# Routing drain and wide attention stage of a two-layer decoder: row positions computed right behind their expert choice, one scatter put ahead of a root, and gathered norms applied ahead of copies

## The chip, the cores and the metric

The kernel runs on one core of one Trainium2 chip. The metric is the device time of one execution in microseconds (us); before the change the median of three runs is 362.25 us. The core's engines work side by side, each with its own queue of instructions in program order: TensorE (PE, matmuls; PEld is its weight load), VectorE (DVE), ScalarE (ACT), GpSimd (POOL) and SyncE (SP, here only for DMAs). They meet through semaphores. An instruction whose semaphore is not there holds up all that stands behind it on its engine.

## The reference, cut to what matters

Two decoder layers over x of 16 sequences of 64 tokens, 128 features: self-attention, cross-attention and a feed-forward block in each, with a residual and a LayerNorm behind each of the six. The first feed-forward block routes every token to two of eight experts:

```python
x = _layernorm(x + _L0_attn_ref(x, ...))       # 16 heads of 8, RoPE, causal
x = _layernorm(x + _L0_xattn_ref(x, ctx, ...)) # 16 heads of 8, masked
x = _layernorm(x + _L0_ffn_ref(x, gate_w, wg, wu, wd))
x = _layernorm(x + _L1_attn_ref(x, W_qkv, W_out))   # 16 heads of 64 ("wide")
x = _layernorm(x + _L1_xattn_ref(x, ctx, ...))
x = _layernorm(x + _L1_ffn_ref(x, ...))        # ternary weights, GELU

def _moe_forward(x, gate_w, wg, wu, wd):       # _L0_ffn_ref, E=8, I=512, K=2
    logits = x_flat @ gate_w.T
    top_v, top_i = jax.lax.top_k(logits, K)
    probs = softmax(top_v)
    combine = einsum('tk,tke->et', probs, one_hot(top_i, E))
    for each expert e:
        hidden = silu(x_flat @ wg[e].T) * (x_flat @ wu[e].T)
        out += combine[e][:, None] * (hidden @ wd[e].T)
```

## The kernel before, in words

The 1024 tokens are eight tiles of 128 tokens (NT = 8), two sequences each. Everything is f32. Each attention stage is a software pipeline over its eight tiles. `stream_pe`, `stream_act`, `stream_dve` and `stream_pool` write, for every step j, what each engine does for the tiles j, j-1, ... j-5 at their different points of the stage. `pre` is the stream of the two first attention stages (a0, a1), `post` the stream of the three last (wide, a2, fc). Between them stands the routed feed-forward block `moe`.

**The drain.** When the stream `pre` is out, the last tiles of cross-attention a1 (S[5], S[6], S[7], the tiles 5 to 7) are finished by four hand-written lists, `drain_pe`, `drain_act`, `drain_dve` and `drain_pool`, in which the first steps of `moe` are woven in. Their order is the order on the engines. For a tile i of a1:

- `va_pe` weighs V with the probabilities (L566, 32 matmuls into the bank B_Y). It waits until `y_dve` of the tile before has read that bank.
- `y_dve` on VectorE makes the reciprocals and normalises y (L676 `rs`, L680 `ysb`).
- `y_pe` transposes y (L582), `y_act` copies it to `yT` on ScalarE (L632), `o_pe` projects it (L586).
- `r_dve` adds the residual (L388 `R`) and takes the statistics (L324, L326 `mv`).
- `rsqrt_pool` makes the root on GpSimd (L331 `ve`, L333 `rstd`); `ln_dve` applies the norm (L337 `X`).
- `moe.x_pe` and `moe.x_act` turn the normed tile into `XT` (L1446, L1450).

Routing goes in groups of two tiles, k = 0 to 3. `logits_pe` and `logits_act` (L1365, L1371) make the expert logits. `choose` on VectorE finds the two best experts (L1379 `top` to L1396 `before`). `rank_pe` counts with small matmuls how many tokens chose each expert before this one (L1412, L1414). `place` on VectorE turns that into the row of each token (L1424 `rk`, L1427 `pm`, L1429 `posf`, L1431 `pos`). `scatter` on GpSimd (L1438) sends a tile's tokens to their rows in the DRAM tensor `routed_rows`, one indirect DMA for each of the two choices, 16 in all. `weights_pe` and `weights_copy` (L1348, L1353) transpose the 24 expert weight blocks in between. The last group's counts give the map of the blocks (`map_dve`, L1464 to L1485).

**The routed block.** SP waits for all 16 scatters, then loads blocks of 128 rows to XG (L1508). Up to 23 blocks go through gate, up and down matmuls (L1550, L1558, L1581). GpSimd then gathers the two rows of each token back (`gather`, L1701, into the memory of KB); `combine` on VectorE adds them to the residual and takes statistics (L1711 to L1719), `rsqrt` on GpSimd makes the root (L1724, L1726), and `apply` on VectorE writes the normed tile (L1731).

**The start of the wide stage.** `combine` and `apply` of the tiles 2 to 7 are put into the first steps of the stream `post` by the hook `post_dve`, and the transposes of these tiles by `post_pe` (`turn_pe`, L1741) and `post_act` (L1747). In step j VectorE does the softmax's maximum and subtraction of tile j-2 (`max_dve`, L403, L409), its share of the copies of Q, K (L877, `qkw_copies`, tile j-1) and V (L877, `vw_copies`, tile j-2) out of PSUM, then the hook, then the rest. TensorE's step is: scores (`s_pe`, L827), projections (`qkw_pe`, L801), V (`v_pe`, L813), the transposes of the probabilities (`t_pe`, L429, which wait for `shares_pool`, L906, on GpSimd), and at the end of the step the hook `turn_pe`.

Of the kernel before, what the change touches and what calls it, by code (L numbers as in the profile page):

```python
# [78 lines left out]
def decoder_kernel(nc, A, out):  # L79
    with ExitStack() as ctx:  # L80
# [1167 lines left out]
        def stream_dve(dve, tiles, extra, last):  # L1248
            for j in range(last):
                y = at(tiles, j - 5)  # L1250
                if y:
                    y.stage.y_dve(dve, y)
                t = at(tiles, j - 3)
                hidden = t and isinstance(t.stage, Ternary)
                if hidden:
                    t.stage.sum_dve(dve, t)
                ternary, others = [], []
                for x in turned(tiles, j):
                    (ternary if isinstance(x.stage, Ternary) else others).append(x)
                for x in others:  # L1260
                    x.stage.ln_dve(dve, x)
                if t and not hidden:
                    t.stage.sum_dve(dve, t)
                v = at(tiles, j - 2)
                if v:
                    v.stage.max_dve(dve, v)
                b, q = at(tiles, j), at(tiles, j - 1)
                if q:
                    q.stage.qkw_copies(dve, 1, q)
                w = at(tiles, j - 4)  # L1270
                if w:
                    w.stage.w_copies(dve, 1, w)
                if v:
                    v.stage.vw_copies(dve, 1, v)
                extra(dve, j, False)
                if w:
                    w.stage.ya_dve(dve, w)
                for r in summed(tiles, j):
                    r.stage.r_dve(dve, r)
                for x in ternary:  # L1280
                    x.stage.ln_dve(dve, x)
                if b:
                    b.stage.qk_dve(dve, b)
                extra(dve, j, True)
# [469 lines left out]
        moe = Routed(a1.norm)  # L1754
# [67 lines left out]
        def drain_pe(pe):  # L1822
            moe.logits_pe(pe, 1)
            a1.y_pe(pe, S[5])
            a1.t_pe(pe, S[7])
            a1.o_pe(pe, S[5])
            a1.va_pe(pe, S[6])
            moe.rank_pe(pe, 1)
            a1.y_pe(pe, S[6])
            weights_pe(pe, 0, 1)  # L1830
            a1.va_pe(pe, S[7])
            a1.o_pe(pe, S[6])
            moe.x_pe(pe, 4)
            weights_pe(pe, 1, 2)
            moe.x_pe(pe, 5)
            weights_pe(pe, 2, 3)
            moe.logits_pe(pe, 2)
            weights_pe(pe, 3, 4)
            a1.y_pe(pe, S[7])
            weights_pe(pe, 4, 5)  # L1840
            a1.o_pe(pe, S[7])
            weights_pe(pe, 5, 7)
            moe.rank_pe(pe, 2)
            moe.x_pe(pe, 6)
            weights_pe(pe, 7, 9)
            moe.x_pe(pe, 7)
            weights_pe(pe, 9, 10)
            moe.logits_pe(pe, 3)
            weights_pe(pe, 10, 13)
            moe.rank_pe(pe, 3)  # L1850
            weights_pe(pe, 13, 3 * EXPERTS)

        def drain_act(act):
            moe.logits_act(act, 1)
            a1.y_act(act, S[5])
            a1.pt_act(act, S[7])
            a1.y_act(act, S[6])
            weights_act(act, 0, 1)
            moe.x_act(act, 4)
            weights_act(act, 1, 2)  # L1860
            moe.x_act(act, 5)
            weights_act(act, 2, 3)
            moe.logits_act(act, 2)
            weights_act(act, 3, 4)
            a1.y_act(act, S[7])
            weights_act(act, 4, 7)
            moe.x_act(act, 6)
            weights_act(act, 7, 9)
            moe.x_act(act, 7)
            weights_act(act, 9, 10)  # L1870
            moe.logits_act(act, 3)
            weights_act(act, 10, 3 * EXPERTS)
            act.activation(warm[:, 0:1], half[:, :], ACT.Silu)

        def drain_dve(dve):
            a1.y_dve(dve, S[5])
            moe.choose(dve, 1)
            a1.r_dve(dve, S[5])
            a1.y_dve(dve, S[6])
            a1.ln_dve(dve, S[4])  # L1880
            moe.place(dve, 1)
            a1.ln_dve(dve, S[5])
            a1.r_dve(dve, S[6])
            a1.y_dve(dve, S[7])
# [6 lines left out]
            moe.place(dve, 3)  # L1891

        def drain_pool(pool):
            a1.rsqrt_pool(pool, S[5])
            moe.scatter(pool, 2, 0)
            moe.scatter(pool, 2, 1)
            a1.rsqrt_pool(pool, S[6])
            moe.scatter(pool, 3, 0)
            moe.scatter(pool, 3, 1)
            a1.rsqrt_pool(pool, S[7])  # L1900
            for t in range(4, NT):
                for r in range(2):
                    moe.scatter(pool, t, r)
# [13 lines left out]
                moe.turn_act(act, TURNED[j, late])  # L1917

        def post_dve(dve, j, late):
            if not late and j in (2, 3):  # L1920
                for t in (2 * j - 2, 2 * j - 1):
                    moe.apply(dve, t)
            if late and j in (1, 2, 3):
                for t in (2 * j, 2 * j + 1):
                    moe.combine(dve, t)
# [153 lines left out]
```

## Time and profile before

| | |
|---|---|
| median of 3 runs | 362.25 us (361.87 to 362.48) |
| the profiled execution | 363.17 us |
| its span, first to last instruction | 361.2 us |
| mean granted TensorE clock | 0.971 |
| TensorE busy | 320.9 us, 89% |
| VectorE busy | 231.3 us, 64% |
| GpSimd busy | 202.8 us, 56% |
| ScalarE busy | 182.7 us, 51% |

Times in the trace count from the span's start. The stages follow each other: the two first attention stages to about 97 us, the drain to about 119 us, the routed block to about 194 us, the gathers and the start of the wide stage to about 229 us, and the rest to 361 us. Busy shares are means over all of them; what a change in one stretch is worth has to be read there, from the wait that ended last.

### The profile page before, as it was taken

How to read it: one execution, taken by the hardware profiler on the slowest of the kernel's cores; microseconds unless marked ns; L12 is line 12 of the kernel's file. 1: busy time of each engine (PE TensorE's matmuls, PEld its weight loads, DVE VectorE, ACT ScalarE, POOL GpSimd, SP SyncE). 2: the span in 40 equal slices, each digit the busy share in tenths (PEclk: the TensorE clock that was granted, in tenths of full speed). 3: DMA queues.
4: the chain of work that ended last, by engine and by line, in shares of the span. 5: the costliest groups of instructions: out<-in, count | busy, mean ns of one | idle time of the engine just before them, and what ended most of it. 6: DMA issues, size and time to landing. Idle time of an engine off the chain costs nothing.

```text
span 361.2 us, 10722 instructions
## 1 busy us (share of the span) xinstructions
PE 320.9 (89%) x4182; PEld 262.6 (73%) x4182; DVE 231.3 (64%) x554; ACT 182.7 (51%) x384; POOL 202.8 (56%) x289
## 2 busy tenths in 40 slices
PE   2969999999888399999995688999999799999993
PEld 2647667777677299999994656798888577767673
DVE  2698987788876023583333379855566667877685
ACT  2457666777558633232322243645444466667651
POOL 2856998887777235553313776422122565476785
PEclk9998999999999789999998599999999999999999
DMA  6799999000011201111101110000000000000001
GB/s 187 224 311 242 296 326 321 14 2 3 24 35 48 62 26 51 47 46 45 44 24 33 43 35 25 4 2 2 4 2 4 3 2 3 4 2 2 2 24 36
DMA packets 37052, 23.55 MB, mean 65 GB/s; under 512 B 4228, under 2 KB 34956, under 8 KB 36876
## 3 DMA queue, kind: packets, MB, share of 16 engines
q1 hardware_dynamic: 35692, 20.16, 19.7%
q0 software_dynamic: 1024, 2.10, 2.0%
q8 instruction: 34, 0.56, 0.6%
q10 hardware_dynamic: 288, 0.62, 0.5%
q14 instruction: 14, 0.11, 0.1%
HBM read 15.13 MB, written 7.73 MB: 63 GB/s over the span
## 4 chain that ended last, share of the span: by engine, by line
PE 73%; DVE 12%; issue 4%; DMA 3%; POOL 3%; ACT 2%; SPq 1%; POOLq 0%; ACTq 0%; DVEq 0%
PE banks L801 8%; PE banks L429 8%; PE banks L1550 6%; PE banks L1558 6%; PE banks L1581 6%; PE banks L566 5%; PE banks L539 5%; PE banks L845 4%; PE banks L813 4%; PE banks L511 3%; PE banks L861 2%; PE banks L523 2%; PE banks L827 2%; PE banks L1026 2%; PE banks L582 2%
## 5 line engine op out<-in xcount | busy, mean ns | idle before, releaser
L690 POOL TENSOR_TENSOR KB<-KT,cst 128x512 f32<-128x512 f32 x48 | 49.3, 1048 | 8.2 <-DVE KT L650 5.9
L438 ACT ACTIVATE PT<-banks 128x512 f32<-128x512 f32 x64 | 34.9, 595 | 24.4 <-PE banks L429 23.2
L403 DVE TENSOR_REDUCE mx<-banks 128x16 f32<-128x1024 f32 x32 | 38.6, 1206 | 11.7 <-PE banks L550 10.1
L1573 DVE TENSOR_TENSOR PT<-banks,PR 128x512 f32<-128x512 f32 x23 | 15.9, 690 | 41.8 <-PE banks L1558 37.5
L1538 POOL COPY U<-WALL 128x1024 f32 x21 | 21.9, 1042 | 36.5 <-PE banks L1558 36.3
L877 ACT ACTIVATE U<-banks 128x512 f32<-128x512 f32 x44 | 26.1, 597 | 30.6 <-PE banks L801 15.3
L331 POOL TENSOR_SCALAR ve<-mv 128x1 f32<-128x1 f32 x40 | 9.2, 230 | 49.4 <-DVE mv L326 49.0
L429 PE MATMUL banks<-cst,PR 128*128 128x128 f32 x256 | 35.5, 283 | 0.6 <-POOL PR L906 0.6
L419 ACT ACTIVATE PR<-PR 128x1024 f32<-128x1024 f32 x32 | 33.8, 1058 | 3.5 <-DVE PR L413 3.2
L801 PE MATMUL banks<-XT,WQKV 128*128 128x128 f32 x256 | 33.0, 291 | 0.4 <-ACT XT L1747 0.4
L801 PEld LDWEIGHTS banks<-XT,WQKV 128*128 128x128 f32 x256 | 31.5, 204 | 1.1 <-ACT XT L1747 0.7
L429 PEld LDWEIGHTS banks<-cst,PR 128*128 128x128 f32 x256 | 28.3, 143 | 4.3 <-POOL PR L906 1.5
L539 PE MATMUL banks<-KB,QS 64*64 64x512 f32 x192 | 27.1, 630 | 3.2 <-DVE PR L413 2.2
L413 DVE TENSOR_TENSOR PR<-banks,mx 128x1024 f32<-128x1024 f32 x24 | 29.4, 1224 | 0.8
L566 PE MATMUL banks<-VB,PT 128*64 128x18 f32 x768 | 26.7, 212 | 0.0
L566 PEld LDWEIGHTS banks<-VB,PT 128*64 128x64 f32 x768 | 24.3, 138 | 3.0 <-issue 0.5
L1550 PE MATMUL banks<-XGT,U 128*128 128x128 f32 x184 | 25.3, 282 | 0.0
L1558 PE MATMUL banks<-XGT,U 128*128 128x128 f32 x184 | 25.1, 281 | 0.0
L1701 POOL DMA_INDIRECT KB<-routed_rows,pos x16 | 15.9, 991 | 16.4 <-DMA routed_rows<-YS 12.3
L333 POOL TENSOR_TENSOR rstd<-ve,half 128x1 f32<-128x1 f32 x40 | 23.1, 578 | 3.3
L1581 PE MATMUL banks<-WALL,PT 128*128 x184 | 24.4, 276 | 0.6 <-DVE YS L1589 0.6
L906 POOL TENSOR_TENSOR PR<-PR,rs 128x1024 f32<-128x1024 f32 x8 | 15.2, 1904 | 17.1 <-DVE rs L916 17.0
(190 smaller groups left out, 722.4 us busy)
## 6 DMA issues: line engine op xcount, KB each, us to landing
routed_rows<-zero SPq DMA_DIRECT2D x1, 4544.0 KB, 21.5
WALL<-in_L_ffn_wg_dram SPq DMA_DIRECT2D x8, 256.0 KB, 5.1
WALL<-in_L_ffn_wu_dram SPq DMA_DIRECT2D x8, 256.0 KB, 5.3
WALL<-in_L_ffn_wd_dram SPq DMA_DIRECT2D x8, 256.0 KB, 5.7
U<-in_L_attn_W_qkv_dram SPq DMA_DIRECT2D x1, 1536.0 KB, 22.8
XG<-routed_rows SPq DMA_DIRECT2D x23, 64.0 KB, 1.8
routed_rows<-YS SPq DMA_DIRECT2D x23, 64.0 KB, 1.6
cst<-shape_constants ACTq DMA_DIRECT2D x1, 537.0 KB, 4.4
```

Source lines behind the costliest of these rows:

```text
L403: dve.tensor_reduce(mx[:, n % 2, :], s, AX.X, ALU.max).then_inc(self.max.sem, 1)
L413: dve.tensor_tensor(PR[:, n % 2, :].rearrange("q (h k) -> q h k", k=SEQ), s, bc(mx[:, n % 2, :], 2, SEQ), ALU.subtract).then_inc(self.sub. ...
L419: act.activation(p, p, ACT.Exp, scale=self.scale).then_inc(self.exp.sem, 1)
L429: t = pe.transpose(PS[:, B_PT + m, P * (r % 4):P * (r % 4 + 1)], PR[:, n % 2, P * r:P * (r + 1)], ident)
L438: act.activation(PT[:, n % 2, 4 * m:4 * m + 4, :].rearrange("p r q -> p (r q)"), PS[:, B_PT + m, :], ACT.Copy).then_inc(self.pt.sem, 1)
L539: pe.matmul(PS[q, B_S + g, :], QS[f, n % 3, q], KB[f, n % 2, b].rearrange("p h k -> p (h k)"), start=True, stop=False)
L566: m = pe.matmul(PS[64 * b:64 * b + 64, B_Y, w * r:w * (r + 1)], PT[:, n % 2, r, 64 * b:64 * b + 64], VB[:, n % 3, r, b].rearrange("p a e - ...
L690: pool.tensor_tensor(KB[:, n % 2, b], bc(KT[:, n % 2, b, :], 1, 8), bc(cst[:, C_HEAD:C_HEAD + 8], 2, SEQ), ALU.mult).then_inc(self.kb.sem, 1)
L801: m = pe.matmul(PS[:, bank, P * k:P * (k + 1)], WQKV[:, f // 2, P * u:P * (u + 1)], XT[:, P * i:P * (i + 1)], start=True, stop=True)
L1550: m = pe.matmul(PS[:, j % 2, P * c:P * (c + 1)], WE[:, j % 3, 0, P * c:P * (c + 1)], XGT[:, j % 3, :], start=True, stop=True)
L1558: m = pe.matmul(PS[:, 2 + j % 2, P * c:P * (c + 1)], WE[:, j % 3, 1, P * c:P * (c + 1)], XGT[:, j % 3, :], start=True, stop=True)
L1581: m = pe.matmul(PS[:, 7, 0:P], HT[:, j % 2, c, :], WALL[:, e, 2, P * c:P * (c + 1)], start=(c == 0), stop=(c == CH - 1))
```

## The change

In the drain, `place(dve, 1)`, the four steps that give the rows of tiles 2 and 3, moves from behind `ln_dve` of tile 4 to directly behind `choose(dve, 1)`. On TensorE `va_pe` of tile 7 moves ahead of `y_pe` of tile 6 and the first weight block; `y_pe` of tile 7 moves one weight block forward, and `rank_pe` of group 2 one weight block forward. ScalarE's list follows. On GpSimd the first scatter of tile 2 moves ahead of the root of tile 5. In the wide stage, `apply` of tiles 2 and 3 (step 2) and 4 and 5 (step 3) moves from behind VectorE's copies to ahead of them, directly behind `max_dve`. No operation is added or removed.

```diff
                 if v:
                     v.stage.max_dve(dve, v)
+                if tiles is post and j in (2, 3):
+                    for g in (2 * j - 2, 2 * j - 1):
+                        moe.apply(dve, g)
                 b, q = at(tiles, j), at(tiles, j - 1)
                 if q:
                     q.stage.qkw_copies(dve, 1, q)
...
             moe.rank_pe(pe, 1)
+            a1.va_pe(pe, S[7])
             a1.y_pe(pe, S[6])
             weights_pe(pe, 0, 1)
-            a1.va_pe(pe, S[7])
             a1.o_pe(pe, S[6])
...
             moe.logits_pe(pe, 2)
-            weights_pe(pe, 3, 4)
             a1.y_pe(pe, S[7])
-            weights_pe(pe, 4, 5)
+            weights_pe(pe, 3, 5)
             a1.o_pe(pe, S[7])
-            weights_pe(pe, 5, 7)
+            weights_pe(pe, 5, 6)
             moe.rank_pe(pe, 2)
+            weights_pe(pe, 6, 7)
...
             a1.y_dve(dve, S[5])
             moe.choose(dve, 1)
+            moe.place(dve, 1)
             a1.r_dve(dve, S[5])
             a1.y_dve(dve, S[6])
             a1.ln_dve(dve, S[4])
-            moe.place(dve, 1)
             a1.ln_dve(dve, S[5])
...
         def drain_pool(pool):
+            moe.scatter(pool, 2, 0)
             a1.rsqrt_pool(pool, S[5])
-            moe.scatter(pool, 2, 0)
             moe.scatter(pool, 2, 1)
...
         def post_dve(dve, j, late):
-            if not late and j in (2, 3):
-                for t in (2 * j - 2, 2 * j - 1):
-                    moe.apply(dve, t)
```

Line numbers of the kernel after the change are 3 higher from the first edit on. VectorE's queue in the drain before, from the end of `choose(1)` (L1396) to the norm of tile 5:

```order
L1396 TENSOR_TENSOR before<-before,chosen 128x8 x2
L388 TENSOR_TENSOR R<-banks,XR 128x128
L324 BN_STATS stats<-R 128x6
L326 BN_AGGR mv<-stats 128x2
L676 RECIPROCAL rs<-banks 128x16
L680 TENSOR_TENSOR ysb<-banks,rs 128x128
L337 TENSOR_SCALAR X<-R,mv,rstd 128x128
L1424 TENSOR_TENSOR rk<-banks,cst 128x16
L1427 TENSOR_TENSOR pm<-OH,rk 128x32
L1429 TENSOR_REDUCE posf<-pm 128x4
L1431 CAST pos<-posf 128x4
L337 TENSOR_SCALAR X<-R,mv,rstd 128x128
```

And after the change:

```order
L1399 TENSOR_TENSOR before<-before,chosen 128x8 x2
L1427 TENSOR_TENSOR rk<-banks,cst 128x16
L1430 TENSOR_TENSOR pm<-OH,rk 128x32
L1432 TENSOR_REDUCE posf<-pm 128x4
L1434 CAST pos<-posf 128x4
L388 TENSOR_TENSOR R<-banks,XR 128x128
L324 BN_STATS stats<-R 128x6
L326 BN_AGGR mv<-stats 128x2
L676 RECIPROCAL rs<-banks 128x16
L680 TENSOR_TENSOR ysb<-banks,rs 128x128
L337 TENSOR_SCALAR X<-R,mv,rstd 128x128 x2
```

The four steps of `place` now stand ahead of the residual of tile 5 and the `ysb` of tile 6. TensorE's queue in the same place before, from the end of `rank_pe(1)` to the transpose of tile 5:

```order
L1414 MATMUL banks<-before,onesb 128x8
L582 MATMUL banks<-cst,ysb 128x128
L1348 MATMUL banks<-cst,WALL 128x128 x4
L566 MATMUL banks<-VB,PT 64x18 x16
L586 MATMUL banks<-WT,yT 128x128
L1446 MATMUL banks<-cst,X 128x128
L1348 MATMUL banks<-cst,WALL 128x128 x4
L1446 MATMUL banks<-cst,X 128x128
```

And after the change:

```order
L1417 MATMUL banks<-before,onesb 128x8
L566 MATMUL banks<-VB,PT 64x18 x16
L582 MATMUL banks<-cst,ysb 128x128
L1351 MATMUL banks<-cst,WALL 128x128 x4
L586 MATMUL banks<-WT,yT 128x128
L1449 MATMUL banks<-cst,X 128x128
L1351 MATMUL banks<-cst,WALL 128x128 x4
L1449 MATMUL banks<-cst,X 128x128
```

The `va_pe` matmuls of tile 7 (L566, 16 in the program, 32 passes in the trace) now stand first. VectorE's queue in step 2 of the stream `post` before, where R and X in L1731 are the residual sums and the normed tiles 2 and 3:

```order
L403 TENSOR_REDUCE mx<-banks 128x16
L409 TENSOR_TENSOR PR<-banks,mx 128x2x8x64
L877 COPY U<-banks 128x512 x2
L1731 TENSOR_SCALAR X<-R,mv,rstd 128x128 x2
L1711 SCALAR_TENSOR_TENSOR R<-KB,pk,X 128x128
```

And after the change:

```order
L403 TENSOR_REDUCE mx<-banks 128x16
L409 TENSOR_TENSOR PR<-banks,mx 128x2x8x64
L1734 TENSOR_SCALAR X<-R,mv,rstd 128x128 x2
L877 COPY U<-banks 128x512 x2
L1714 SCALAR_TENSOR_TENSOR R<-KB,pk,X 128x128
```

The two norms change places with the two copies.

## Rows read from the trace of the kernel before

**Rows 1.** The page: the span, and engines' busy time with share and instructions.

```profile
span 361.2 us, 10722 instructions
PE 320.9 (89%) x4182; PEld 262.6 (73%) x4182; DVE 231.3 (64%) x554; ACT 182.7 (51%) x384; POOL 202.8 (56%) x289
```

**Rows 2.** The chain that ended last, drain: start us, us, what.

```profile
99.15 0.30 DVE R L388
...
100.16 0.30 DVE ysb L680
...
101.28 1.04 PE banks L566 x32
102.32 0.42 PE banks L586 x2
...
113.71 0.26 DVE pos L1431
...
118.09 2.21 DMA routed_rows<-X,pos
```

**Rows 3.** The timeline, 98 to 103 us: start, us, engine, line, operation [idle before].

```profile
99.43 0.17 PE L1414 MATMUL banks<-before,onesb 128*128 128x8 bf16 x1
100.51 0.33 PE L582 MATMUL banks<-cst,ysb 128*128 128x128 f32 x1 [0.92 <-DVE ysb L680]
100.74 0.17 DVE L1424 TENSOR_TENSOR rk<-banks,cst 128x16 f32<-128x16 f32 x1
100.88 0.37 ACT L632 ACTIVATE yT<-banks,bvc 128x128 f32<-128x128 f32 x1 [2.01 <-PE banks L582]
101.48 0.34 DVE L337 TENSOR_SCALAR X<-R,mv,rstd 128x128 f32<-128x128 f32 x1
102.83 0.29 DVE L388 TENSOR_TENSOR R<-banks,XR 128x128 f32<-128x128 f32 x1 [1.02 <-PE banks L586]
```

**Rows 4.** The timeline of GpSimd in the drain.

```profile
100.08 0.22 POOL L331 TENSOR_SCALAR ve<-mv 128x1 f32<-128x1 f32 x1 [0.41 <-DVE mv L326]
...
101.86 1.09 POOL L1438 DMA_INDIRECT routed_rows<-X,pos  x1 [0.91 <-DVE pos L1431]
...
107.94 0.28 POOL L331 TENSOR_SCALAR ve<-mv 128x1 f32<-128x1 f32 x1 [0.26 <-DVE mv L326]
...
114.30 0.96 POOL L1438 DMA_INDIRECT routed_rows<-X,pos  x1 [0.30 <-DVE pos L1431]
```

**Rows 5.** Stretches: busy (x count) of PE, PEld, DVE, ACT, POOL, PEclk, DMA, GB/s.

```profile
26.00:28.00 2.00, 2.00 (x17) 1.58 (x14) 1.97 (x4) 0.76 (x3) 2.00 (x3) 0.50 1.13 312
...
126.00:128.00 2.00, 2.00 (x11) 2.00 (x11) 0.00 (x0) 0.60 (x1) 0.00 (x0) 0.50 0.11 33
128.00:130.00 2.00, 2.00 (x19) 2.00 (x18) 0.69 (x1) 0.79 (x2) 1.04 (x1) 0.93 0.00 0
```

**Rows 6.** The timeline of TensorE behind two of its gaps.

```profile
24.77 1.09 PE L539 MATMUL banks<-KB,QS 64*64 64x512 f32 x8 [2.17 <-DVE PR L413]
...
286.83 0.29 PE L845 MATMUL banks<-WOUT,U 128*64 128x128 f32 x1 [1.89 <-issue]
```

**Rows 7.** The timeline at the start of the wide stage.

```profile
212.28 1.22 DVE L409 TENSOR_TENSOR PR<-banks,mx 128x1024 f32<-128x1024 f32 x1
...
216.33 0.59 DVE L1731 TENSOR_SCALAR X<-R,mv,rstd 128x128 f32<-128x128 f32 x2
216.84 0.35 DVE L1711 SCALAR_TENSOR_TENSOR R<-KB,pk,X 128x128 f32<-128x128 f32 x1
217.03 0.41 PE L1741 MATMUL banks<-cst,X 128*128 128x128 f32 x2 [1.35 <-issue]
...
219.42 0.22 POOL L1724 TENSOR_SCALAR ve<-mv 128x1 f32<-128x1 f32 x1 [0.20 <-DVE mv L1719]
...
222.82 1.91 POOL L906 TENSOR_TENSOR PR<-PR,rs 128x1024 f32<-128x1024 f32 x1
...
224.79 1.09 PE L429 MATMUL banks<-cst,PR 128*128 128x128 f32 x8 [0.62 <-POOL PR L906]
```

More of the change, by code:

```diff
@@ L1863, in drain_act @@
             moe.logits_act(act, 2)
-            weights_act(act, 3, 4)
             a1.y_act(act, S[7])
-            weights_act(act, 4, 7)
+            weights_act(act, 3, 7)
             moe.x_act(act, 6)
```

## The prediction, made before the result was known

> **What bounds the kernel now.** I read the page's busy shares first [rows 1]: TensorE is busy 89% of 361.2 us, so over most of the span any saving elsewhere is hidden. The change touches two short stretches, so I then read the chain that ended last in the drain, and the timelines of the engines there and at the start of the wide stage.
>
> In the drain the chain does not run along TensorE. It is a loop over four engines. VectorE ends `choose(1)` and takes the residual sum R of tile 5 at 99.15 and its statistics, then makes `ysb` of tile 6 (to 100.46); TensorE weighs V of tile 7 (101.28 to 102.32) and projects tile 6 (`o_pe`, from 102.32) [rows 2]. From there it goes over tile 5's logits, `choose(2)`, the residual of tile 7, its root on GpSimd, its logits, `choose(3)` and `place(3)`, which ends at 113.97 [rows 2]. The last of the 16 scatters starts at 118.09 [rows 2], and SP's block loads wait for it.
>
> GpSimd's queue runs beside this loop, and I looked at whether it is a second bound. It waits 0.91 for the rows of tile 2 at 101.86, but later 0.26 for the statistics of tile 7 at 107.94, and its scatter of tile 6 starts at 114.30, 0.33 behind the rows of `place(3)` [rows 2, 4]. So the queue and the loop reach 114 us level. Later the queue is full: 114.30 to 118.09 is four scatters of 1.26. Two consequences: a faster GpSimd queue alone gains nothing, since `place(3)` holds the scatter of tile 6, and a later loop moves all behind it.
>
> In the wide stage TensorE waits 1.35 ahead of the transposes of tiles 2 and 3 at 217.03, which need the norms that VectorE made at 216.33, behind its copies. It waits again, 0.62, at 224.79 for GpSimd's shares, which start at 222.82 [rows 7]. From there it is nearly always busy.
>
> **The drain, step by step.** The four steps of `place(1)` need TensorE's counts, ready at 99.60 (99.43 + 0.17) [rows 3]. They took 0.74 of VectorE's queue (100.74 to 101.48) [rows 3]. Before, they lay behind `ysb` and in a time in which VectorE then stood idle for 1.02 anyway, ahead of the residual of tile 6 at 102.83 [rows 3]: they cost nothing. After, VectorE waits to 99.63 and does them to 100.37, and only then R of tile 5, which began at 99.15: 1.22 later. From R to the end of `ysb` nothing else enters, so `ysb` of tile 6 is there at 101.68 instead of 100.46.
>
> TensorE now has V of tile 7 first. It waits for the same `ysb` (B_Y must be read), so it cannot use the gap, it starts at about 101.73. It takes 1.04 [rows 2], to 102.77; `y_pe` of tile 6 takes 0.33, ScalarE's copy of it 0.37 [rows 3], so `o_pe` starts at 102.77 + 0.33 + 0.37 and two hand-overs of 0.04 to 0.05 (100.51 + 0.33 to 100.88 is such a one [rows 3]): 103.56. Before it was 102.32 [rows 2]. The new order on TensorE adds 0.02 to the 1.22; the copy that was hidden behind V now lies bare, but V no longer stands between it and the projection. **Sum: +1.24.**
>
> What of this reaches the end? Behind `o_pe` everything up to `place(3)` has the same order in both kernels as far as it binds. The root of tile 5 starts later (behind the early scatter, about 101.75 instead of 100.08 [rows 4]), and its norm is done by 103.0; tile 5's transpose, which needs it, would come at about 104.5, so it is covered by 1.5. `y_pe` of tile 7 comes one weight block earlier, but the residual of tile 7 stands behind `choose(2)` on VectorE, which does not get earlier. The statistics of tile 7, for which GpSimd waits at 107.94 [rows 4], come at 109.1; `place(3)` ends at 115.2, the last scatter starts at 119.3. The weight blocks (L1348) of the end of the drain stand behind `rank_pe(3)` and move with it.
>
> The early scatter itself: it waits for rows at 100.54 (place's end, 0.17 behind its last start) and starts about 100.8 instead of 101.86. It brings the queue at most 1.06, all of which the queue loses again waiting for the statistics of tiles 6 and 7. Bounds: 0 to -1.06, taken at 0, as the row at 107.94 already shows a wait for the loop, not for the queue. Bounds of the drain: from -0.3 (the queue decides alone and only its own 0.26 goes) to +1.3.
>
> **The wide stage, step by step.** Ahead of the copies, the norms of tiles 2 and 3 run behind the subtraction that ends at 213.50 (212.28 + 1.22) [rows 7]. TensorE's transposes lose their wait of 1.35 [rows 7]. What is late next? The shares at 222.82 [rows 7]. They stand in GpSimd's queue behind the last gathers, behind the roots of tiles 4 and 5 (219.42, 0.20 behind VectorE's statistics). VectorE's `combine` of tile 4 started at 216.84, behind the two norms that began at 216.33 [rows 7]; with these gone it starts when the copy ahead is written, 0.4 to 0.5 earlier. All the rest of that path, statistics, root, gathers, shares, `t_pe` at 224.79, moves by this much. So the transposes' 1.35 shrinks to **-0.42**, and TensorE's wait for the shares grows from 0.62 to about 1.5. The same move for tiles 4 and 5 hides behind that: their transposes at step 3's end stand behind `t_pe` in any case. The copies come 0.6 later for the norms ahead; they free banks for projections 3 us later, cost nothing. Bounds: 0 (if the copy is what `combine` waits for) to -1.35.
>
> **The sum.** +1.24 - 0.42 = +0.82. Against the profiled execution's 363.17 (span 361.2 and 1.97 around it) this is 363.99. That execution lay 0.92 above the median of 362.25; carried to the median it is 363.07, and I say 363.1.
>
> **The clock.** The granted clock is 0.50 at 126 to 128 us and 0.93 over 128 to 130 [rows 5]: the first blocks of the routed block run at the lower of the two levels, 1.2 instead of 2.4 GHz, since TensorE stood idle before the first rows came. If the return stays where it is in time, work that begins 1.2 later spends 1.2 less at half speed, and gives back 0.6. If it moves with the work, nothing comes back. The rows of one execution can't tell the two. The Trainium skill (TensorE: Matmul & The Clock Gate, Part 1: The HAM clock gate) says that the monitor runs free and doesn't start anew with a kernel; by that the return isn't tied to the kernel's work, and 0.6 come back in some executions and not in others. This trace can't show it.
>
> **The rivals.**
> - *The clock gives back part* (above): 363.1 - 0.6 = 362.5.
> - *The clock falls in the drain.* TensorE's gap behind the counts grows from 0.92 to 2.1 (99.60 to 101.73). A gap of 2.17 at 24.77 was followed by a granted clock of 0.50 at 26 to 28 us, one of 1.89 at 286.83 was not [rows 5, 6]. If it falls, some 2 to 3 us of TensorE's work on the loop (projection, transposes, logits) runs at half speed. I bound that from 0 to +2 and take +1: 364.1. The same could happen in the wide stage, where the gap is 1.5; less likely.
> - *The wide stage gives all of its 1.35*, if the shares' path shortens more than I see, by VectorE's earlier copies of statistics: 362.25 + 1.24 - 1.35 = 362.1.
> - *Faster: the scatters decide.* If VectorE's new order kept the residual of tile 6 at 102.83, the loop would not move, and the queue's 1.06 at the scatter of tile 2 would count up to the point where `place(3)` stops it. It decides if `ysb` of tile 6 is ready by about 100.9. Price: -0.3 to -1.06, say -0.5, with -0.42 of the wide stage 361.3. Against it stands that the counts alone hold `place(1)` to 99.60, 0.45 behind the moment at which R had begun [rows 2, 3].
>
> **How the numbers follow.** Forecast 0.50 at 363.1; clock gives back 0.15 (362.5); clock falls 0.15 (364.1); wide stage gives all 0.10 (362.1); scatters decide 0.10 (361.3). About 0.2% of this kernel, 0.7 us, is what a measurement can tell from no change, so 362.97 is the border to slower and 361.53 to faster. The forecast lies 0.1 above the upper border, and the three runs before span 0.6: of its 0.50 I count 0.35 as slower and 0.15 as the same. Slower: 0.35 + 0.15 = 0.50. Same: 0.15 + 0.15 + 0.08 = 0.38, the rest of the wide stage's case and the scatters' case, 0.12, faster. Low end: below the two cases at 362.1 and 362.5 with the runs' spread, 361.9. High end: the clock case at 364.1 and 0.2, 364.3. Left out is the scatters' case and the tail of the clock case.
>
> **What would show it.** Right, if in the profile after: VectorE's L1427 starts near 99.6 and R of tile 5 near 100.4; `o_pe` of tile 6 starts near 103.6; the last scatter near 119.3, with GpSimd waiting ahead of the root of tile 7 as before. In the wide stage the first two transposes follow V without a wait, and `t_pe` waits about 1.5 for the shares, near 225.6 (224.79 + 1.24 - 0.42). Wrong, if the last scatter starts at 118.1 or sooner: then the loop was not what bound the drain. Wrong in size, if the granted clock is 0.50 anywhere between 100 and 110 us, or if the stretch at 0.50 in the routed block is shorter or longer than before.

## The result and the profile after

The changed kernel takes 365.68 us in the median of six runs (364.06 to 366.32). The kernel before, run beside it six times, takes 362.52 us (361.87 to 363.64). The ratio is 1.0069, with a 95% interval of 1.0044 to 1.0093: slower by 2.5 us (0.0069 x 362.52), with 1.6 to 3.4 as the interval; the two medians lie 3.16 apart, inside it. A few executions of the kernel before, of e2 and of e6 below were over 1.5% slower than the fastest of their kernel, at a lower clock: the medians include them, the ratios don't. I had forecast 363.1 and a range up to 364.3. The direction was right, the size was not: the loss is about three times the +0.82 of the sum.

The page of the changed kernel, its lines as in [rows 1]:

```profile
span 362.1 us, 10722 instructions
PE 319.9 (88%) x4182; PEld 262.7 (73%) x4182; DVE 232.7 (64%) x554; ACT 182.7 (50%) x384; POOL 203.0 (56%) x289
```

The span is only 0.9 us longer than the 361.2 of [rows 1]. The profiled execution is the quickest of the six (364.06), so it must not be read as the typical one. Therefore I measure stretches, each from a landmark inside itself. The drain is measured from the start of the V matmuls of tile 6, which both kernels have in the same place. They stand in the timeline of TensorE, of before and then of after (start, us, engine, line, operation, forms, [idle before <-releaser]):

```profile
98.28 1.11 PE L566 MATMUL banks<-VB,PT 128*64 128x18 f32 x32
```

```profile
97.26 1.11 PE L566 MATMUL banks<-VB,PT 128*64 128x18 f32 x32
```

The changed kernel came into the drain 1.02 earlier, though nothing ahead of it was changed. The reason is in the stretch of [rows 5] at 26 to 28 us, here of after (columns as in [rows 5], the granted clock stands third from the right):

```profile
26.00:28.00 2.00, 2.00 (x24) 1.65 (x24) 1.97 (x3) 1.58 (x5) 2.00 (x3) 1.00 1.13 310
```

Before, the clock was 0.50 there; in this execution it stayed at 1.00. Nothing of the change stands ahead of this stretch, and the kernels below show both clocks in it whatever they keep of the change. So I read it as a difference of executions and not of kernels. It flattered the changed kernel's profile by about 1 us.

**The drain.** The chain that ended last in the changed kernel, to be laid beside [rows 2] (start, us, what):

```profile
100.83 1.11 PE banks L566 x32
...
103.20 0.43 PE banks L586 x2
...
115.16 0.25 DVE pos L1434
...
119.53 2.23 DMA routed_rows<-X,pos
```

From V of tile 6 to the last scatter it was 19.81 before (98.28 to the 118.09 of [rows 2]) and is 22.27 now (97.26 to 119.53): **+2.46**. The timeline shows where it starts, of all engines:

```profile
98.62 0.17 DVE L1427 TENSOR_TENSOR rk<-banks,cst 128x16 f32<-128x16 f32 x1 [0.42 <-PE banks L1417]
...
99.38 0.29 DVE L388 TENSOR_TENSOR R<-banks,XR 128x128 f32<-128x128 f32 x1
...
100.39 0.29 DVE L680 TENSOR_TENSOR ysb<-banks,rs 128x128 f32<-128x128 f32 x1
...
100.83 1.11 PE L566 MATMUL banks<-VB,PT 128*64 128x18 f32 x32 [2.25 <-DVE ysb L680]
...
102.14 1.06 PE L1351 MATMUL banks<-cst,WALL 128*128 128x128 f32 x4
...
103.00 0.64 PE L586 MATMUL banks<-WT,yT 128*128 128x128 f32 x2
...
103.72 0.29 DVE L388 TENSOR_TENSOR R<-banks,XR 128x128 f32<-128x128 f32 x1 [1.60 <-PE banks L586]
```

VectorE now waits 0.42 for the counts, makes the rows, and only then R of tile 5 and `ysb` of tile 6. TensorE stands idle for 2.25 ahead of V of tile 7; before, its gap at this place was 0.92, ahead of the transpose of tile 6 [rows 3]. Then something comes that [rows 3] don't have: four transposes of a weight block take 1.06. Before they took 0.60:

```profile
100.68 0.60 PE L1348 MATMUL banks<-cst,WALL 128*128 128x128 f32 x4
```

The stretches of after say why:

```profile
100.00:102.00 2.00, 1.17 (x33) 1.17 (x34) 1.09 (x6) 0.00 (x0) 1.70 (x4) 0.96 0.10 33
102.00:104.00 2.00, 2.00 (x10) 1.99 (x11) 0.40 (x2) 1.09 (x3) 0.96 (x1) 0.50 0.10 33
104.00:106.00 2.00, 2.00 (x13) 1.78 (x12) 0.92 (x5) 1.31 (x4) 1.07 (x3) 0.69 0.00 0
```

The granted clock fell to 0.50, the lower of the two levels (1.2 GHz), for 102 to 104 us and part of the next stretch. Before, this stretch ran at full speed:

```profile
102.00:104.00 2.00, 2.00 (x24) 1.55 (x20) 1.06 (x5) 0.95 (x3) 1.70 (x2) 1.00 0.10 33
```

The 10 matmuls here and the 24 before can't be compared one by one, since the 24 include the short ones at the end of V. The weight block can: the same four transposes, 1.06 against 0.60.

GpSimd's queue after, which answers to [rows 4]:

```profile
99.72 0.96 POOL L1441 DMA_INDIRECT routed_rows<-X,pos  x1 [1.06 <-DVE pos L1434]
...
109.37 0.28 POOL L331 TENSOR_SCALAR ve<-mv 128x1 f32<-128x1 f32 x1 [1.29 <-DVE mv L326]
...
115.74 0.96 POOL L1441 DMA_INDIRECT routed_rows<-X,pos  x1 [0.30 <-DVE pos L1434]
```

What the early scatter brought the queue is lost again at the root of tile 7: GpSimd waits 1.29 there, before 0.26 [rows 4].

**The wide stage.** The timeline after, which answers to [rows 7]:

```profile
214.36 0.59 DVE L1734 TENSOR_SCALAR X<-R,mv,rstd 128x128 f32<-128x128 f32 x2
...
223.26 1.91 POOL L906 TENSOR_TENSOR PR<-PR,rs 128x1024 f32<-128x1024 f32 x1
...
223.41 2.11 DVE L1734 TENSOR_SCALAR X<-R,mv,rstd 128x128 f32<-128x128 f32 x2
...
225.22 1.09 PE L429 MATMUL banks<-cst,PR 128*128 128x128 f32 x8 [1.45 <-POOL PR L906]
...
225.44 1.28 DVE L877 COPY U<-banks 128x512 f32<-128x512 f32 x2
```

From the first scores of the stage to `t_pe` (L429) it was 15.91 (208.88 to 224.79) and is 15.40 (209.82 to 225.22): the norms of tiles 2 and 3 at 214.36 take 0.59, as they did behind the copies. `combine` of tile 4 behind them comes 0.51 earlier (7.45 behind the first scores, before 7.96), and with it the shares and `t_pe`. The norms of tiles 4 and 5 at 223.41 take **2.11** for the same two instructions. They lie beside GpSimd's multiplication by the shares (L906, 223.26 to 225.17), and one of the two norms took nearly all of it. All norms of this line (duration in ns as minimum, median, maximum):

```profile
L1734 DVE TENSOR_SCALAR X<-R,mv,rstd x8: 335/346/1855, 201.5 to 230.2; 128x128 f32<-128x128 f32 x8
```

The copies behind them wait to 225.44, and all that follows in VectorE's queue is late with them, down to three copies that start 8.95 behind `t_pe` (234.17), before 8.07 (232.86). TensorE's first output projection waits for one of those (timeline of TensorE, after):

```profile
235.71 0.29 PE L845 MATMUL banks<-WOUT,U 128*64 128x128 f32 x1 [0.99 <-DVE U L877]
```

From `t_pe` to this row it was 10.03 (to 234.82) and is 10.49. So the wide stage gains 0.51 and gives back 0.46.

### The profile page after: what moved, and what is told of

Read it like the earlier page. It is cut to its first block, busy times and chain, and to the rows that moved or that the text cites. A ratio compares the mean times of both kernels' runs of the same rounds, so it can differ in the third digit from the quotient of the medians.

```text
span 362.1 us, 10722 instructions
## 1 busy us (share of the span) xinstructions
PE 319.9 (88%) x4182; PEld 262.7 (73%) x4182; DVE 232.7 (64%) x554; ACT 182.7 (50%) x384; POOL 203.0 (56%) x289
## 4 chain that ended last, share of the span: by engine, by line
PE 70%; DVE 17%; issue 5%; DMA 3%; POOL 2%; ACT 2%; SPq 1%; POOLq 0%; DVEq 0%; ACTq 0%
PE banks L429 8%; PE banks L801 7%; PE banks L1553 6%; PE banks L1561 6%; PE banks L1584 6%; PE banks L566 5%; PE banks L539 5%; PE banks L845 4%; PE banks L813 3%; PE banks L511 3%; PE banks L523 2%; PE banks L861 2%; DVE mx L403 2%; PE banks L1026 2%; PE banks L827 2%
## 5 line engine op out<-in xcount | busy, mean ns | idle before, releaser
L429 PE MATMUL banks<-cst,PR 128*128 128x128 f32 x256 | 34.9, 279 | 1.4 <-POOL PR L906 1.4
L429 PEld LDWEIGHTS banks<-cst,PR 128*128 128x128 f32 x256 | 27.6, 141 | 5.1 <-POOL PR L906 2.3
L566 PE MATMUL banks<-VB,PT 128*64 128x18 f32 x768 | 26.7, 212 | 2.3 <-DVE ysb L680 2.2
L566 PEld LDWEIGHTS banks<-VB,PT 128*64 128x64 f32 x768 | 24.4, 138 | 5.2 <-issue 2.7
L906 POOL TENSOR_TENSOR PR<-PR,rs 128x1024 f32<-128x1024 f32 x8 | 15.2, 1904 | 17.1 <-DVE rs L916 17.1
```

The source lines that it names most:

```text
L429: t = pe.transpose(PS[:, B_PT + m, P * (r % 4):P * (r % 4 + 1)], PR[:, n % 2, P * r:P * (r + 1)], ident)
L566: m = pe.matmul(PS[64 * b:64 * b + 64, B_Y, w * r:w * (r + 1)], PT[:, n % 2, r, 64 * b:64 * b + 64], VB[:, n % 3, r, b].rearrange("p a e - ...
```

## The experiments

My theory was the sum of the prediction: VectorE's place ahead of the residual costs the drain 1.24, and the rest is the clock that falls behind TensorE's longer gap. The rivals were: TensorE's new order or the early scatter is what costs; the wide stage loses. All kernels are named by what they keep of the change. The table has the drain in microseconds behind the start of V of tile 6: `ysb` of tile 6, R of tile 6, R of tile 7 and the last scatter, worked out from each trace's timeline. Then the time against the kernel before.

| kernel | ysb 6 | R 6 | R 7 | last scatter | clock under 1.00 between 100 and 108 | ratio, 95% |
|---|---|---|---|---|---|---|
| before | 1.88 | 4.55 | 8.73 | 19.81 | no | |
| after | 3.13 | 6.46 | 11.18 | 22.27 | yes | 1.0069 (1.0044 to 1.0093) |
| e1, drain alone | 3.12 | 6.31 | 11.06 | 22.14 | yes | 1.0094 (1.0067 to 1.0121) |
| e5, e1 with TensorE's old order | 3.13 | 5.84 | 10.91 | 21.94 | yes | 1.0077 (1.0058 to 1.0095) |
| e11, e1 without the early scatter | 3.13 | 6.29 | 11.06 | 22.14 | yes | 1.0092 (1.0054 to 1.0130) |
| e8, e1 with work moved into the gap | 3.13 | 6.23 | 11.25 | 22.76 | yes | 1.0094 (1.0067 to 1.0121) |
| e10, e1 with useless work in the gap | 3.13 | 5.98 | 10.39 | 21.47 | no | 1.0053 (1.0032 to 1.0074) |
| e6, TensorE's order alone | 1.89 | 4.74 | 8.93 | 20.01 | no | 1.0026 (0.9998 to 1.0055) |
| e7, early scatter alone | 1.88 | 5.86 | 9.41 | 20.49 | no | 1.0042 (1.0027 to 1.0058) |
| e2, e3, e4, e9 (wide stage only) | | | | 19.80 to 19.81 | no | 0.9984 to 1.0008 |

The times against the kernel before come out longer than the drain's loss in each of the kernels with a change in the drain alone, by 0.3 to 1.1: for e1 3.4 against 2.33, for e7 1.5 against 0.68, and in these two the low end of the interval (2.4 and 1.0) still lies above it. Each trace is of one execution, and where this rest lies is not shown. From the last scatter to the first scores of the wide stage it takes 90.29 to 91.30 in the six profiles with the rows early (mean 90.75) and 89.78 to 90.79 in the seven others (mean 90.36); whether that 0.4 belongs to the change or to chance, one profile of each can't tell.

### Drain alone, wide stage alone

e1 is the changed kernel with the norms of the wide stage back behind the copies:

```diff
-                if tiles is post and j in (2, 3):
-                    for g in (2 * j - 2, 2 * j - 1):
-                        moe.apply(dve, g)
...
         def post_dve(dve, j, late):
+            if not late and j in (2, 3):
+                for t in (2 * j - 2, 2 * j - 1):
+                    moe.apply(dve, t)
```

> The drain part of the change alone, the wide stage as before. Theory A (the loop over VectorE and TensorE is 1.24 us longer, and TensorE's gap of 2.25 us behind the counts lets the clock fall to 1.2 GHz in the drain, another 1.1 us in executions where it does): slower by 1.2 to 2.4 us, last scatter about 2.4 us later against TensorE's entry into the drain when the granted clock is 0.50 there, 1.2 when it is not. Rival B (the wide part holds most of the loss of the whole change, 3.2 us): slower by 0.5 us or less.

Measured: 365.59 us, the whole loss of the changed kernel. The drain takes 22.14, the clock falls again (stretches; this execution came into the drain at 98.51, 1.25 later than after's):

```profile
102.00:104.00 2.00, 1.93 (x37) 1.93 (x38) 0.53 (x2) 0.37 (x1) 1.72 (x3) 0.83 0.09 33
104.00:106.00 2.00, 2.00 (x11) 2.00 (x10) 1.07 (x5) 1.04 (x3) 0.41 (x2) 0.50 0.10 33
```

e2 is the other half, the kernel before with the norms ahead of the copies in steps 2 and 3 (the same diff with its signs turned).

> The wide part alone (norms of tiles 2 to 5 ahead of the copies), the drain as before. Theory A: the norms of step 3 lie beside GpSimd's multiplication by the shares, take 2.1 us instead of 0.6, and the copies behind them come 2.5 us later; what step 2 gained (0.4 to 0.5 at the first transposes of probabilities) is lost again by the first wide output projection: net 0 to +0.5 us. My prediction on record: -0.42. Rival B: +1.5 us or more.

Measured: 362.75 us, ratio 1.0008 (0.9988 to 1.0028). So the loss is in the drain, and the wide part is worth nothing that can be timed. In its trace the 15.91 fell to 15.39, and the 10.03 rose to 10.48, as in after.

### The wide stage, step by step

e3 moves the norms of step 2 alone, e4 those of step 3 alone:

```diff
+                if tiles is post and j in (2,):
+                    for g in (2 * j - 2, 2 * j - 1):
+                        moe.apply(dve, g)
...
-            if not late and j in (2, 3):
+            if not late and j in (3,):
```

> Only the norms of tiles 2 and 3 (step 2) go ahead of the copies. Theory A: they lie beside a gather, not beside the multiplication; 0.59 us for the two as before, first transposes of probabilities 0.4 to 0.5 earlier, kept to the end: -0.4 us. Rival (nothing of this is kept): 0.

> Only the norms of tiles 4 and 5 (step 3) go ahead of the copies. Theory A: 2.1 us for the two norms beside the multiplication, copies later by 2.5, the output projection of the first wide tile 0.4 to 1 us later: +0.4 to +1 us. If the long norm is a chance of one execution: 0.59 us for the two and no change of time.

Measured: e3 362.41 us, 0.9995 (0.9975 to 1.0015); e4 362.69 us, 0.9998 (0.9973 to 1.0024). The times can't part them, the traces do. e3 has the gain alone (15.39, then 10.03), e4 the loss alone (15.91, then 10.48). Timeline of e4, VectorE and GpSimd:

```profile
221.27 1.91 POOL L906 TENSOR_TENSOR PR<-PR,rs 128x1024 f32<-128x1024 f32 x1
...
221.42 2.11 DVE L1734 TENSOR_SCALAR X<-R,mv,rstd 128x128 f32<-128x128 f32 x2
```

And of e3, where the norms stand behind the copies and meet only the end of the multiplication:

```profile
221.91 1.91 POOL L906 TENSOR_TENSOR PR<-PR,rs 128x1024 f32<-128x1024 f32 x1
222.07 1.28 DVE L877 COPY U<-banks 128x512 f32<-128x512 f32 x2
...
223.26 0.91 DVE L1734 TENSOR_SCALAR X<-R,mv,rstd 128x128 f32<-128x128 f32 x2
```

The multiplication ends at 223.82. The first norm starts at 223.26, takes 0.65 instead of 0.35 and ends at 223.91, 0.09 behind the multiplication; the second takes its 0.34. Together they make the 0.91. In after the long norm (223.41, 1.86) ends 0.10 behind the multiplication. Alone the pair takes 0.59 [rows 7]. The copies out of PSUM, which run beside the multiplication for nearly its whole length here, take 1.28, as they do at 225.44 in after, where it is over. So it is the norm, out of SBUF and into SBUF, that is held until GpSimd's instruction ends, not every instruction of VectorE. The Trainium skill (SBUF — State Buffer, Who interferes with whom) states this as a rule: VectorE and GpSimd share a pair of ports, a `tensor_scalar` can run in a mode that takes it, and "Whoever issues first gets the shared pair for the whole instruction". The traces agree: 0.35 becomes 1.86 in after and 1.85 in e2 and in e4.

e9 tests that reading. It keeps step 2 early and puts the norms of step 3 still further ahead, in front of the maximum, where GpSimd isn't yet at its multiplication:

```diff
                 if t and not hidden:
                     t.stage.sum_dve(dve, t)
+                if tiles is post and j == 3:
+                    for g in (2 * j - 2, 2 * j - 1):
+                        moe.apply(dve, g)
                 v = at(tiles, j - 2)
                 if v:
                     v.stage.max_dve(dve, v)
+                if tiles is post and j in (2,):
+                    for g in (2 * j - 2, 2 * j - 1):
+                        moe.apply(dve, g)
...
```

> The drain as before. Norms of step 2 ahead of the copies as in the change; norms of step 3 moved still further up, ahead of the maximum, where GpSimd issues a gather and not yet the multiplication by the shares. If the collision with the multiplication is what made the pair 2.1 us long: 0.6 us here, first transposes of probabilities 15.4 us behind the first scores (before 15.9), first output projection 10.0 us behind them (10.5 in the change): -0.5 us in all. If the early place itself makes them long: 2.1 us again and no gain.

Its timeline, VectorE, GpSimd and TensorE:

```profile
219.13 0.51 DVE L1737 TENSOR_SCALAR X<-R,mv,rstd 128x128 f32<-128x128 f32 x2
...
221.32 1.91 POOL L906 TENSOR_TENSOR PR<-PR,rs 128x1024 f32<-128x1024 f32 x1
...
221.95 1.28 DVE L877 COPY U<-banks 128x512 f32<-128x512 f32 x2
...
223.28 1.09 PE L429 MATMUL banks<-cst,PR 128*128 128x128 f32 x8 [1.45 <-POOL PR L906]
```

Measured: the norms take 0.51, the stretches are 15.39 and 10.04, so the 0.52 of step 2 is kept and nothing is given back. The time is 361.92 us, 0.9984 (0.9964 to 1.0005). It beats the changed kernel. Against the kernel before the gain of 0.52 lies inside the interval, so it is shown by the trace and not by the time.

### Which part of the drain costs

e5 is e1 with the lists of TensorE and ScalarE of before. e6 is the opposite, the kernel before with these two lists of after. The start of the difference on TensorE, from e1 to e5:

```diff
             moe.rank_pe(pe, 1)
-            a1.va_pe(pe, S[7])
             a1.y_pe(pe, S[6])
             weights_pe(pe, 0, 1)
+            a1.va_pe(pe, S[7])
             a1.o_pe(pe, S[6])
...
```

> The drain part with TensorE's and ScalarE's order as before: only VectorE's place and GpSimd's scatter are moved. Theory A (VectorE's place ahead of the residual is what costs): the ysb of tile 6 is 1.24 us late here too, TensorE's gap behind the counts is 2.2 us, the clock falls: as slow as the drain part alone, +2.4 us or more. Rival C (TensorE's V of tile 7 ahead of the transpose of tile 6 is what costs): back to within 0.5 us of before.

> Only TensorE's and ScalarE's order of the change in the drain, VectorE and GpSimd as before. Theory A: gap behind the counts 0.92 to 1.0 us, clock at 1.00, the projection of tile 6 within 0.1 us of before: 0 us. Rival C: +1 us or more.

Measured: e5 364.75 us and a drain of 21.94, e6 363.17 us (1.0026, with 1 inside the interval) and 20.01. So TensorE's new order costs 0.20 of its own, and without it the loss is nearly all there. In e5 the gap stands ahead of the transpose of tile 6 (timeline):

```profile
100.76 0.33 PE L582 MATMUL banks<-cst,ysb 128*128 128x128 f32 x1 [2.16 <-DVE ysb L680]
```

and the clock falls to 0.50 at 104 to 106 (0.70 in the 2 us ahead of it). In e6 the gap is 1.01 and the clock stays at 1.00:

```profile
100.45 1.11 PE L566 MATMUL banks<-VB,PT 128*64 128x18 f32 x32 [1.01 <-DVE ysb L680]
```

e7 is the kernel before with the early scatter alone, e11 is e1 without it:

```diff
         def drain_pool(pool):
+            moe.scatter(pool, 2, 0)
             a1.rsqrt_pool(pool, S[5])
-            moe.scatter(pool, 2, 0)
             moe.scatter(pool, 2, 1)
```

> Only the scatter of tile 2 ahead of the root of tile 5 on GpSimd, all else as before. The scatter then waits for rows that VectorE has at 101.6, the root comes 2.8 us later, the norm of tile 5 at 103.8, and the residual of tile 6 behind it on VectorE at about 104.2 instead of 102.83: +1.0 to +1.4 us at the last scatter, clock at 1.00. Rival (GpSimd's order is free, as in the change): 0 us.

> The drain part alone with GpSimd's order as before (root of tile 5 ahead of both scatters of tile 2). If VectorE's place ahead of the residual is all that counts: 22.2 us from V of tile 6 to the last scatter as in the drain part, clock 0.50 in it. If the early scatter costs or gains anything behind the early place: away from 22.2 by the 0.7 us that it cost alone.

Measured: e7 363.53 us, 1.0042 (1.0027 to 1.0058); e11 365.45 us, 1.0092 (1.0054 to 1.0130). The early scatter alone is bad: GpSimd waits for the rows of tile 2 while the root of tile 5 stands behind the scatter, and VectorE waits for that root (timeline of e7, GpSimd and VectorE):

```profile
101.64 0.96 POOL L1438 DMA_INDIRECT routed_rows<-X,pos  x1 [2.17 <-DVE pos L1431]
...
103.56 0.35 DVE L337 TENSOR_SCALAR X<-R,mv,rstd 128x128 f32<-128x128 f32 x1 [2.19 <-POOL rstd L333]
```

It costs 0.68 in the drain (20.49 against 19.81), less than the 1.0 to 1.4 that I had expected: R of tile 6 is 1.31 late, and R of tile 7 only 0.68. With the rows early it costs nothing and gains nothing: e1 and e11 are both at 22.14. The term that I had put at 0 is 0, as far as one profile of each shows.

### The clock

e1's order delays `ysb` of tile 6 by 1.25, but its last scatter by 2.33. If the clock accounts for the rest, a TensorE that doesn't stand idle should save it. e8 moves two weight blocks into the gap, e10 fills it with 16 transposes whose output nobody reads:

```diff
             moe.rank_pe(pe, 1)
+            weights_pe(pe, 0, 2)
             a1.va_pe(pe, S[7])
             a1.y_pe(pe, S[6])
-            weights_pe(pe, 0, 1)
             a1.o_pe(pe, S[6])
             moe.x_pe(pe, 4)
-            weights_pe(pe, 1, 2)
...
```

```diff
+        def fill_pe(pe, n):
+            pe.wait_ge(s_raw, 48 * EXPERTS)
+            pe.wait_ge(*pre[-1].s_read())
+            for _ in range(n):
+                for c in range(CH):
+                    pe.transpose(PS[:, 0, P * c:P * (c + 1)], WALL[:, 0, 0, P * c:P * (c + 1)], ident)
...
             moe.rank_pe(pe, 1)
+            fill_pe(pe, 4)
             a1.va_pe(pe, S[7])
```

> The drain part of the change, with the weight blocks 0 and 1 (0.9 us of TensorE) moved into TensorE's gap, ahead of V of tile 7. Theory A: the gap shrinks from 2.25 to about 1.3 us, the granted clock stays at 1.00 in the drain, and the last scatter comes 1.2 us later than before instead of 2.4: 1.1 us faster than the drain part alone, and still 1.2 us slower than before. Rival D (the second 1.2 us is not the clock but the order): as slow as the drain part alone.

> The drain part alone, with TensorE's order of the change, and in its gap of 2.25 us 16 further transposes of the first weight block into the bank that this block gets anyway (1.8 us of work for nothing; nothing waits for it and the output is the same). The run before this one, with 0.9 us of weight work moved into the gap, still had a granted clock of 0.50 and was no faster, so that moving work doesn't settle it. Theory A (the second 1.1 us of the drain is the clock): granted clock 1.00 from 100 to 108 us, from the start of V of tile 6 to the last scatter 21.1 us instead of 22.2, and 1.1 us faster than the drain part alone. Rival D (it is the order): 22.2 us here too.

e8 measured 364.93 us and a drain of 22.76, no better than e1. The gap is shorter, and the clock fell all the same (timeline and stretches of e8):

```profile
98.46 1.06 PE L1348 MATMUL banks<-cst,WALL 128*128 128x128 f32 x8
...
100.79 1.11 PE L566 MATMUL banks<-VB,PT 128*64 128x18 f32 x32 [1.26 <-DVE ysb L680]
```

```profile
102.00:104.00 2.00, 1.13 (x5) 0.60 (x4) 0.60 (x3) 0.65 (x2) 0.91 (x1) 0.68 0.10 33
104.00:106.00 2.00, 2.00 (x10) 2.00 (x11) 0.68 (x4) 0.91 (x3) 1.34 (x3) 0.50 0.00 0
```

The weight blocks that now fill the gap are missing behind V, where TensorE is busy only 1.13 of 2 us. Part of the idle time was moved rather than removed. So e8 refutes the simple form of my theory, that the length of the one gap decides, and leaves the clock itself untested, since it fell in e8 too.

e10 tests it. TensorE is busy through the gap and all else is e1 (timeline, then the stretch):

```profile
98.68 1.94 PE L1827 MATMUL banks<-cst,WALL 128*128 128x128 f32 x16
...
101.00 1.11 PE L566 MATMUL banks<-VB,PT 128*64 128x18 f32 x32 [0.39 <-DVE ysb L680]
...
102.21 0.60 PE L1348 MATMUL banks<-cst,WALL 128*128 128x128 f32 x4
```

```profile
102.00:104.00 2.00, 1.98 (x18) 1.53 (x16) 0.84 (x3) 1.34 (x4) 1.09 (x1) 1.00 0.09 33
```

Measured: the clock stays at 1.00 over all of the drain, the weight block takes 0.60 again, V starts 0.43 behind `ysb` as in e1, and the drain is 21.47 instead of 22.14 (I had expected 21.1). The time is 364.35 against e1's 365.59. More work for TensorE, and 1.24 us less time; what differs in the drain's stretches is the clock. In the drain it is worth 0.67 against e1 and 0.80 against after; the rest of the 1.24 lies outside the drain or between executions, and the two ratios' intervals meet (1.0067 and 1.0074), so I take the number from the traces, of which there is one each.

With the clock out, e10 still has +1.66 over before. The table splits it: 1.25 at `ysb` of tile 6; 0.18 more at R of tile 6, which e6 shows as the price of TensorE's order (4.74 against 4.55); 0.23 more at R of tile 7 (from R of tile 6 to R of tile 7 it takes 4.41 in e10, and 4.18 before and 4.19 in e6). The last has no experiment, but the trace has its place. In e10 the norm of tile 6, just ahead of this R, took 0.57 where it takes 0.34 to 0.38 elsewhere, and it ended with a scatter's issue on GpSimd:

```profile
106.81 0.96 POOL L1438 DMA_INDIRECT routed_rows<-X,pos  x1 [0.30 <-issue]
...
107.22 0.57 DVE L337 TENSOR_SCALAR X<-R,mv,rstd 128x128 f32<-128x128 f32 x1
```

The same length turns up where nothing was changed: in e4, e5, e7 and e10 the second norm of the pair of tiles 2 and 3 starts some 0.4 behind the start of a gather's issue, takes 0.56 and ends just behind it, so that the pair takes 0.81 or 0.82 (timeline of e4):

```profile
214.60 0.94 POOL L1704 DMA_INDIRECT KB<-routed_rows,pos  x1 [0.30 <-issue]
214.78 0.81 DVE L1734 TENSOR_SCALAR X<-R,mv,rstd 128x128 f32<-128x128 f32 x2
```

In before, e1, e6, e8 and e11 the pair lies in the same place and takes 0.59. So a norm beside such an issue took some 0.22 longer in five cases and not in the others; why is open. After's own norm of tile 6 took 0.34 and was not held. Without this hold e10's drain would be 21.24 (an estimate, 21.47 less 0.23), and the clock's share in after is then 1.03 (22.27 less 21.24). Taken directly, e10 against after, it is 0.80.

## Why the prediction was wrong

By its own steps, each as forecast and as measured:

| term | forecast | measured | by |
|---|---|---|---|
| rows of tiles 2, 3 ahead of R and `ysb` | +1.22 | +1.25 | after, e1, e10 |
| TensorE's new order | +0.02 | +0.18 | e6, e10 |
| on to R of tile 7 | 0 | 0 to +0.23 | after's norm was not held, e10's was |
| clock in the drain | 0, a rival with 0.15 | +1.03 to +0.80 | e10 against after |
| early scatter | 0 | 0 | e11 against e1 |
| norms of tiles 2, 3 | -0.42 | -0.51 | after, e3 |
| norms of tiles 4, 5 | 0 | +0.46 | after, e4 |
| sum | +0.82 | +2.41 | ratio: +2.5 |

**What held.** The loop over four engines is what bounds the drain, and VectorE's queue is where the change enters it. The wait for the counts, R of tile 5 after it and `ysb` 1.22 later came as worked out. The queue of GpSimd is no second bound: what it gained it waited off ahead of tile 7's root, as forecast. In the wide stage the shares at GpSimd limit what early norms can bring, `t_pe` waits 1.45 where I said 1.5, and the gain is near the 0.42. The rival that the scatters decide is gone, and so is the one that the wide stage gives all of its 1.35.

**The step that failed most** is the one on the clock. I saw that TensorE's gap would grow to 2.1, laid it between a gap of 2.17 with a fall and one of 1.89 without [rows 5, 6], priced the fall at +1, and then gave it 0.15 and left it out of the sum. The price was right (0.80 to 1.03). The chance was not: in the drain the clock fell in all four profiles that have the rows early and the gap open (after, e1, e5, e11), and in e8. The nearest row was the one with the fall, and 2.1 is three times nearer to it than to the other (0.07 against 0.21; the measured 2.25 lies beyond both). By that the fall should have been in the forecast and no fall the rival: 363.1 + 1 = 364.1. Two things temper this. The row at 24.77 was itself near a toss: behind the same gap the clock fell in 7 of 13 profiles, which one trace couldn't show. And 364.1 is still below the 365.68 measured: the terms of the table on 362.52 give 364.93, and the remaining 0.75 lies inside the interval and has no place in the traces.

**The step on the norms of tiles 4 and 5** failed too: "hides behind that" looked only at who needs these norms, and "the copies come 0.6 later ... cost nothing" only at their own length. I did not look at what runs on GpSimd at the place to which they were moved. There stood the multiplication by the shares, 1.91 long [rows 7], and the norm waits for its end. Its own move costs 0.46, almost all that step 2 gains. The row to look at was in [rows 7] itself: at 222.82 the multiplication starts, about when VectorE would come to the norms.

**TensorE's order** was mis-sized by 0.16: V of tile 7 does not start 0.05 behind the end of `ysb` but 0.15 (100.01 + 0.29 to 100.45 in e6), and the chain and the timeline put the old start of `o_pe` 0.07 apart (102.32 [rows 2], 102.25 in the timeline).

**The clock of the routed block** gave nothing back in any way that can be told from chance. From the last scatter to the last copy of the block it takes 73.53 before, 73.11 to 73.76 in the six kernels with the rows early, and 72.74 to 74.30 in the others.

## What to carry to other kernels

Before an instruction is moved forward on an engine of a loop that is the bound, count what then stands behind its wait: here two instructions of the loop stood behind a wait for counts that had been hidden, and the loop is late by all of it. Then look at the engine at the other end, since a gap that grows there may also cost its clock, and work moved into the gap helps only if none is missing later. For a VectorE instruction that reads and writes SBUF, look also at GpSimd's timeline at the new place: a norm of 0.35 took 1.86 beside a multiplication that had begun just ahead of it.

## What the runs showed that I had not expected

The same gap is not followed by the same clock. All thirteen profiles have the gap of [rows 6] at 24.5 to 25.0 us, 2.17 to 2.19 long. In seven of them, the kernel before among them, the clock was 0.50 to 0.58 at 26 to 28 us; in the six others, after among them, it was 1.00. The drain is entered at 97.18 to 97.44 us in the six and at 98.08 to 98.99 in the seven. The Trainium skill (TensorE: Matmul & The Clock Gate, Part 1: The HAM clock gate) says that the monitor of the clock runs free and doesn't start with the kernel; a fall in some executions and not in others agrees with that, and no run here shows the monitor itself. Why the drain's fall came in all five profiles with the rows early and no idle work, even in e8 with a gap of 1.26, is open.

Work that computes nothing made a kernel quicker: 16 transposes in a gap, 1.94 us of TensorE's time, gave 0.67 us back in the drain. It is still slower than the kernel before (1.0053).
